# Graph layer on one core: edge tiles of 128 rows in place of 125, another first stage, whole scans over the edges' targets

## The chip, the cores and the metric

The kernel runs on one core of one Trainium2 chip. The metric is the device time of one execution in microseconds, the median of several runs.

## The reference

x is 6250 x 512, with 100,000 edges (src, dst) that are sorted by dst, and dst is dense at low numbers (the square of a uniform number). All is float32.

```python
xn = _layernorm(x, axis=-1)
# graph attention, 8 heads of 64
el = einsum('nhf,hf->nh', xn @ W_src + b_src, attn_l)
er = einsum('nhf,hf->nh', xn @ W_dst + b_dst, attn_r)
e = leaky_relu(el[src] + er[dst], 0.2)
a = exp(e - segment_max(e, dst)[dst]) / segment_sum(...)[dst]
gnn = segment_sum((xn @ W_val + b_val)[src] * a, dst)
# linear attention with random features: Q_phi, K_phi, V from xn @ Wq, Wk, Wv
mix = (Q_phi @ (K_phi^T V)) / (Q_phi @ sum(K_phi)) @ Wo
x = x + gnn + mix
# experts, top 781 tokens of each of 8 experts, after 8 Sinkhorn steps
out = x + ffn(_layernorm(x, axis=-1), gate_w, experts)
```

## The kernel before

Nodes lie in 50 tiles of P = 125; partition p of tile t holds node 50 p + t where tables are written by `by_tile`. Edges lie in ET = 800 tiles of 125, in sorted order. The stages, in order:

1. **First stage.** x comes in G = 25 groups of two tiles into six buffers (NXI). DVE takes mean and variance and normalizes, PE transposes into `xnT_all`, and multiplies by `welr`, the two logit weights folded with attn_l and attn_r (`fold_logit_weights` on DVE). Before the fold PE spreads four parameter rows over all partitions (`rows_spread`, L656 to L658). The logits el go to DRAM by group (`store_el`, L385 on SP's queue). SP loads the first six groups of x and the even ones after that (`load_x`, L379); ACT's queue loads the odd ones (L981). POOL meanwhile looks up where each node's edges begin (L537). `first_edge`, `all_edges` and `first_row` on DVE turn that into rows of the edge table; `first_row` needs one column moved by one partition, which a DMA on SP's queue does (L411, `starts_moved`), behind the loads of the projection weights (L398 to L406).
2. **Attention.** `group` on PE: 25 groups of projections (k, v, q, the graph values), feature maps and the sum over keys, and the values go to `val_tab` in DRAM (520 floats a row, 64 values and a one for each head). Then come the fold of Wo, the division (`divide`) and the output (`output`).
3. **Logit gathers.** Beside all this POOL issues one indirect DMA for each edge tile (`gather_logits`, L552): row src of `el_tab` to the partition of its edge. Edges are regarded as NCH = 16 chunks of CL = 6250, each of CT = 50 tiles; a gather goes to `ELP[:, g, c, :]`, for tile g of chunk c, and the order is by blocks of TB = 4 values of g (64 gathers), the last block first, NB = 13 blocks. After the first five blocks come 50 scatters of the er logits to the rows of `er_starts` where each node's edges begin (L565).
4. **Scans.** With the blocks turned by PE (`turn_block`), 128 partitions hold chunk and head, and 6250 columns the edges of a chunk. DVE copies the targets and compares neighbours (L1380, L1383), spreads er along equal targets by a scan (L1395), prepares two masks (L1398, L1400), all in 13 pieces, and then, block by block as logits come, adds, takes the leaky relu and the running maximum backwards (L1409 to L1414). A second pass (L1444 to L1447) subtracts the maximum, ACT takes the exponent, and PE turns the weights back to edge tiles.
5. **Edge loop.** POOL gathers `val_tab` rows for tile after tile into a ring of RING = 32 slots (`gather_pair`, L594), and reports a pair when it has landed, three pairs behind (`report`, L600, BEHIND = 3). DVE multiplies by the weights (`messages`, L1452 and L1463), ACT makes one-hot matrices of the targets (L1110, L1113), PE multiplies both (`block_sums`, L640) and sums into one of two accumulators for each of the 50 node blocks. `pairs` holds the pair at which a block ends; that pair is taken by both blocks. After each block come its gates (`gates`), a transpose (L892), the loading of the other two terms (`load_xm`) and a store (`store_x1`).
6. **Experts.** Sinkhorn, the choice of tokens, and 56 slots of 112 rows: an indirect read (L618), a product, an indirect write (L627).

```python
for u in range(ET // 2):
    eng.wait_ge(S["tile_free"], 2 * u + 2)
    gather_pair(u)
    if u >= BEHIND:
        report(u - BEHIND)
```

`chunk(...)`, `two(...)` and `mm(...)` are helpers for addresses in PSUM and matmuls; most matmuls carry the line of `mm`, L640.

## Time and profile before

| | us |
|---|---|
| median of 3 runs | 3210.87 (3203.05 to 3212.89) |
| profiled execution, its own time | 3184.74 |
| its span | 3182.6 |
| PE busy | 2569.4 |
| POOL busy | 2209.5 |
| DVE busy | 1621.1 |
| ACT busy | 993.6 |
| mean granted clock of PE | 0.907 |

The busy times are sums over the span and say little of what a stage waits for. The chain of waits follows the last instruction back to what released it, step by step; the windows give the busy time of each engine in each stage; the groups of lines give the mean of one instruction; and the rows of the timeline give each start and duration, with the idle time before it and what ended it.

### The profile page before, as it was taken

To read this page: it belongs to the slowest core of one execution; us is meant where nothing else is said; L and a number is where in the kernel's file an instruction comes from. 1 tells how busy PE (TensorE), PEld (TensorE's weight loads), DVE (VectorE), ACT (ScalarE), POOL (GpSimd) and SP (SyncE) were. 2 spreads that over 40 slices of the span, in tenths; PEclk is the share of its full clock that TensorE was granted. 3 is DMA by queue.
4 is the path that set the end of the run, shared out by engine and by line. 5 is a ranking of instruction groups with operands and counts; after the bars stand their busy time and mean duration, and the time that the engine had idled before them with its cause. 6 is when DMAs were issued, how large, how long until landed. Compare 5 with 4: busy or idle time off the path is not lost.

```text
span 3182.6 us, 47522 instructions
## 1 busy us (share of the span) xinstructions
PE 2569.4 (81%) x10463; PEld 1790.9 (56%) x10464; DVE 1621.1 (51%) x2963; ACT 993.6 (31%) x2564; POOL 2209.5 (69%) x1847
## 2 busy tenths in 40 slices
PE   6689999999999989951676777777888988934998
PEld 3366677776677744420454556665666766723443
DVE  6612222222222269985854555555666666767232
ACT  2312222222222210020454444554555655600111
POOL 6287778777778777877877877777777777600454
PEclk9889999999999989985699998898988999955999
DMA  4341121111111133420566667777777777630111
GB/s 144 122 105 33 31 37 29 29 29 29 30 31 29 23 105 119 117 64 3 157 174 173 176 181 183 185 186 182 194 193 187 196 193 195 175 111 0 45 52 38
DMA packets 276032, 341.23 MB, mean 107 GB/s; under 512 B 164855, under 2 KB 184030, under 8 KB 275850
## 3 DMA queue, kind: packets, MB, share of 16 engines
q0 software_dynamic: 218672, 227.51, 31.6%
q1 hardware_dynamic: 51709, 93.57, 9.1%
q10 hardware_dynamic: 5594, 19.52, 1.7%
q8 instruction: 20, 0.33, 0.0%
q14 instruction: 37, 0.30, 0.0%
HBM read 285.65 MB, written 55.25 MB: 107 GB/s over the span
## 4 chain that ended last, share of the span: by engine, by line
POOL 41%; PE 19%; issue 16%; DMA 13%; DVE 8%; DVEq 2%; POOLq 0%; ACT 0%; ACTq 0%
POOL R L552 31%; PE ps L640 17%; DMA R<-val_tab,src_i 11%; POOL R L594 8%; POOL er_starts L565 2%; DMA work<-in_x_dram 1%; DVEq L239 1%; DVE R L1463 1%; DVE work L1557 1%; DMA R<-in_L_gnn_b_dst_dram 1%; PE ps L934 1%; DVEq L1463 1%; PE ps L664 1%; DVE R L1444 0%; DVE R L1500 0%
## 5 line engine op out<-in xcount | busy, mean ns | idle before, releaser
L640 PE MATMUL ps<-R,work 125*125 (+3 forms) x5240 | 1650.6, 470 | 225.7 <-DVE R L1463 207.2
L640 PEld LDWEIGHTS ps<-R,work 125*125 125x125 f32 (+2 forms) x5240 | 987.6, 195 | 795.0 <-issue 655.7
L552 POOL DMA_INDIRECT R<-el_tab,src_i x800 | 984.6, 1231 | 341.1 <-issue 288.7
L594 POOL DMA_INDIRECT R<-val_tab,src_i x800 | 978.7, 1223 | 280.7 <-issue 180.8
L1463 DVE TENSOR_TENSOR R<-R,ps (+1 forms) x800 | 521.2, 693 | 131.4 <-DVE ps L1452 125.6
L1113 ACT ACTIVATE work<-work 125x125 f32<-125x125 f32 x900 | 277.8, 309 | 500.0 <-PE ps L640 472.1
L640 PE MATMUL ps<-work,R 128*128 128x250 f32 x1600 | 359.5, 383 | 21.8 <-DMA work<-R 21.8
L1110 ACT ACTIVATE work<-work,negdst 125x125 f32<-125x125 f32 x900 | 353.6, 393 | 59.2 <-issue 34.5
L640 PEld LDWEIGHTS ps<-work,R 128*128 128x128 f32 x1600 | 308.9, 194 | 59.1 <-issue 21.8
L1452 DVE COPY ps<-R (+1 forms) x401 | 69.9, 175 | 299.2 <-POOLq L600 227.1
L1295 DVE TENSOR_TENSOR R<-ps,R 125x512 f32<-125x512 f32 x50 | 34.6, 692 | 358.1 <-PE ps L640 358.1
L618 POOL DMA_INDIRECT R<-out_dram,work x56 | 55.7, 994 | 196.7 <-DVEq L1630 179.9
L1342 DVE RECIPROCAL work<-ps 128x1000 f32<-128x1000 f32 x25 | 160.0, 6402 | 13.0 <-PE ps L640 12.9
L640 PE MATMUL ps<-R 128*128 (+6 forms) x524 | 133.1, 402 | 26.8 <-DVEq L1626 13.6
L1166 ACT ACTIVATE work<-ps 128x448 f32<-128x448 f32 x56 | 30.4, 544 | 337.3 <-PE ps L934 337.3
L640 PEld LDWEIGHTS ps<-R 128*128 128x128 f32 (+3 forms) x524 | 83.3, 166 | 74.5 <-issue 34.6
L627 POOL DMA_INDIRECT out_dram<-R,work x56 | 54.0, 965 | 97.7 <-DVE R L1646 97.7
L1646 DVE SCALAR_TENSOR_TENSOR R<-ps,work,R 112x512 f32<-112x512 f32 x56 | 42.1, 751 | 149.8 <-PE ps L640 149.8
L1302 DVE TENSOR_SCALAR work<-ps 125x512 f32<-125x512 f32 x50 | 34.6, 692 | 157.1 <-PE ps L640 157.1
L1028 ACT ACTIVATE work<-ps 125x512 f32<-125x512 f32 x50 | 29.9, 597 | 246.5 <-PE ps L640 246.5
L640 PE MATMUL ps<-work 125*128 125x129 f32 (+1 forms) x500 | 74.1, 287 | 39.8 <-issue 38.4
L640 PE MATMUL ps<-omk,work 128*125 128x128 f32 x400 | 87.1, 309 | 21.4 <-DVE work L1303 21.4
(256 smaller groups left out, 2186.0 us busy)
## 6 DMA issues: line engine op xcount, KB each, us to landing
work<-in_x_dram SPq DMA_DIRECT2D x33, 500.0 KB
R<-el_tab,src_i POOLq DMA_INDIRECT x800
R<-val_tab,src_i POOLq DMA_INDIRECT x800, 5.9
val_tab<-R SPq DMA_DIRECT2D x50, 253.9 KB
work<-R SPq DMA_DIRECT2D x25, 500.0 KB
work<-xm_tab SPq DMA_DIRECT2D x50, 250.0 KB
out_dram<-R SPq DMA_DIRECT2D x50, 250.0 KB
xm_tab<-work ACTq DMA_DIRECT2D x17, 500.0 KB
```

The costliest lines, as they stand in the source:

```text
L552: eng.indirect_dma_start(out=ELP[:, g, c, :], out_offset=None, in_=el_tab[:, :], in_offset=bass.IndirectOffsetOnAxis(ap=src_i[:, t:t + 1], ...
L565: eng.indirect_dma_start(out=er_starts[:, :], out_offset=bass.IndirectOffsetOnAxis(ap=slot_s[:, t:t + 1], axis=0), in_=elr_all[:, 1, t, :] ...
L594: eng.indirect_dma_start(out=ring[:, slot, :], out_offset=None, in_=val_tab[:, :], in_offset=bass.IndirectOffsetOnAxis(ap=src_i[:, 2 * u + ...
L618: eng.indirect_dma_start(out=xs[q], out_offset=None, in_=out[:, :], in_offset=bass.IndirectOffsetOnAxis(ap=xs_tok[:, n:n + 1], axis=0), bo ...
L627: eng.indirect_dma_start(out=out[:, :], out_offset=bass.IndirectOffsetOnAxis(ap=xs_tok[:, n:n + 1], axis=0), in_=ys[q], in_offset=None, bo ...
L640: return pe.matmul(o, l, r, start=start, stop=stop)
L1110: fn(absd[s][0:P, :], iota_f[0:P, :], ACT.Abs, bias=negdst[:, bass.ds(2 * u + s, 1)]).then_inc(S["act_step"], 1)
L1113: fn(onehot[s][0:P, :], absd[s][0:P, :], ACT.Relu, scale=-1.0, bias=1.0).then_inc(S["onehot_ready"], 1)
L1342: st.done(v.reciprocal(rq.rearrange("p (b n) -> p b n", b=2), two(2 * b)))
L1452: v.tensor_copy(weights2[:, bass.ds(u % WPAIRS, 1), :].rearrange("p a h -> p (a h)"), EW2[:, bass.ds(u, 1), :].rearrange("p a h -> p (a h) ...
L1463: v.tensor_tensor(out=r3, in0=r3, in1=w_, op=ALU.mult).then_inc(S["msg_ready"], 1)
L1646: v.scalar_tensor_tensor(out=ys[m % NX], in0=ps[0:SLOT, 6 + m % 2, :], scalar=of_slot(2, n), in1=x_, op0=ALU.mult, op1=ALU.add).then_inc(S ...
```

## The change

- Edge tiles have B = 128 rows. A chunk has CT = 49 tiles and CL = 6272 edges, so that there are NT = 784 tile places, of which NE = 782 hold edges; the last two are skipped by the gathers. The last tile's empty rows have index 0 for src and no target. All tiles of stages 3 to 5 become 128 high. Node tiles stay at 125.
- `src_i` and `dst_i` arrive in another layout. The host's copy of src is for tiles of 125, so the indices are loaded on ACT's queue, cast, turned by PE, kept by DVE (`keep_rows`), written to DRAM (`src_nat`), read back as 112 rows of 896, turned by PE again (`turn_rows`) and kept. The targets are read from dst in 112 rows of 896 and turned by PE after the fold of Wo.
- The first stage: all x loads are on SP's queue; the parameter rows are loaded as broadcasts to 128 partitions on ACT's queue, and PE no longer spreads them; `first_edge` of the first half stands after three trips of six groups in place of two. The first row of each chunk and the gate weights are loaded on ACT's queue at the start. The zero fill of `er_starts` and the targets are loaded ahead of the one-column DMA.
- The scan of er and the two masks are one operation each over 6272 columns in place of 13 pieces.
- Attention's third buffer for x (NXM = 3) stays as it was.

```diff
-CL = E // NCH
-CT = CL // P
+B = 128
+CT = -(-E // (NCH * B))
+CL = CT * B
+NT = NCH * CT
+EQ = NT * B
+NE = -(-E // B)
+NI = 7
+NR = NT // NI
+REST = E - (NR - 1) * NI * B
...
             for g in range(NXI):
                 load_x(g)
+
+            eng.wait_ge(S["consts_ready"], 2)
+            eng.wait_ge(S["edge_rows"], 4)
+            n_ = (NI - 1) * 128 * P
+            eng.dma_start(src_nat[0:n_].rearrange("(j p n) -> p j n", p=128, n=P), src_turned[:, 0:NI - 1, :]).then_inc(S["idx_loaded"], 16)
+            eng.dma_start(src_nat[n_:E].rearrange("(p n) -> p n", n=P), src_turned[0:(E - n_) // P, NI - 1, :]).then_inc(S["idx_loaded"], 16)
+            eng.dma_start(src_nat[E:EQ].rearrange("(p n) -> p n", p=1), blank[0:1, 0:EQ - E]).then_inc(S["idx_loaded"], 16)
+            eng.wait_ge(S["idx_loaded"], 64)
+            eng.dma_start(src_rows, src_nat.rearrange("(p n) -> p n", p=NR)).then_inc(S["idx_loaded"], 16)
...
                 eng.dma_start(w_q, Wq.rearrange(wv4, p=128)).then_inc(S["proj_params"], 16)
+                eng.dma_start(er_starts.rearrange("(p a r) h -> p a (r h)", p=128, a=16),
+                              blank.unsqueeze(1).to_broadcast([128, 16, CT * H])).then_inc(S["er_zeroed"], 16)
+                eng.wait_ge(S["edge_psum"], 2)
+                eng.dma_start(dst_i[0:NR - 1, :], dst[0:E - REST].rearrange("(p n) -> p n", n=NI * B)).then_inc(S["heads_in"], 16)
+                eng.dma_start(dst_i[NR - 1:NR, 0:REST], dst[E - REST:E].rearrange("(p n) -> p n", p=1)).then_inc(S["heads_in"], 16)
...
                     for c in range(NCH):
                         t = c * CT + g
+                        if t >= NE:
+                            continue
...
-            for u in range(ET // 2):
+            for u in range(NE // 2):
                 eng.wait_ge(S["tile_free"], 2 * u + 2)
...
+            pe.wait_ge(S["edge_rows"], 7)
+            turn_rows(negdst_rows, 4)
...
-                        m = mm(halves_of[0], onehot[s][0:P, :], row[:, 0:DV // 2], False, stop)
+                        m = mm(halves_of[0], onehot[s], row[:, 0:DV // 2], False, stop)
...
-            for k in range(NB):
-                lo, hi = columns(k)
-                st.done(v.tensor_tensor_scan(out=scan_x[:, lo:hi], data0=scan_p[:, lo:hi], data1=scan_m[:, lo:hi],
-                                             initial=0.0 if k == 0 else scan_x[:, lo - 1:lo], op0=ALU.mult, op1=ALU.add))
-
-                st.done(v.tensor_scalar(scan_p[:, lo:hi], scan_p[:, lo:hi], -1.0, -FAR, ALU.add, ALU.mult))
-
-                st.done(v.tensor_scalar(scan_d[:, lo:hi], scan_d[:, lo:hi], ends[:, 2:3], FAR, ALU.subtract, ALU.mult))
+            st.done(v.tensor_tensor_scan(out=scan_x, data0=scan_p[:, 0:CL], data1=scan_m, initial=0.0, op0=ALU.mult, op1=ALU.add))
+
+            st.done(v.tensor_scalar(scan_p[:, 0:CL], scan_p[:, 0:CL], -1.0, -FAR, ALU.add, ALU.mult))
```

SP's queue at the start, before: eight loads of x, then stores of el between the even loads.

```order
L379 DMA work<-in_x_dram 125x1024 x8
L385 DMA el_tab<-negdst 125x16
L379 DMA work<-in_x_dram 125x1024
L385 DMA el_tab<-negdst 125x16 x2
L379 DMA work<-in_x_dram 125x1024
```

The same in the change:

```order
L396 DMA work<-in_x_dram 125x1024 x6
L410 DMA src_nat<-dst_i 128x6x125
L411 DMA src_nat<-dst_i 32x125
L412 DMA src_nat<-R 1x352
L414 DMA dst_i<-src_nat 112x896
L396 DMA work<-in_x_dram 125x1024 x4
L402 DMA el_tab<-negdst 125x16
```

The way of src through DRAM now stands between the sixth and the seventh load, and every later load of x is behind it.

SP's queue between the first stage and attention, before (`tb<-tb` is the one-column DMA, `work<-R` a group for PE):

```order
L406 DMA R<-in_L_mix_Wq_dram 128x4x512
L411 DMA tb<-tb 124x1
L417 DMA work<-R 128x4x250
L427 DMA gw<-in_L_ffn_gate_w_dram 128x4x8
L428 DMA smi<-in_dst_dram 16x1
L429 DMA dst_i<-in_dstT_dram 125x800
L430 DMA er_starts<-R 2000x1x400
```

The same in the change:

```order
L432 DMA R<-in_L_mix_Wq_dram 128x4x512
L433 DMA er_starts<-R 2048x1x392
L436 DMA dst_i<-in_dst_dram 111x896
L437 DMA dst_i<-in_dst_dram 1x544
L442 DMA tb<-tb 124x1
L448 DMA work<-R 128x4x250 x2
```

The zero fill and the targets moved from behind the one-column DMA and the first group to ahead of both.

## Rows read from the trace of the kernel before

**Rows 1.** The page, part 4: the chain that ended last, by engine and by line.
```profile
POOL 41%; PE 19%; issue 16%; DMA 13%; DVE 8%; DVEq 2%; POOLq 0%; ACT 0%; ACTq 0%
POOL R L552 31%; PE ps L640 17%; DMA R<-val_tab,src_i 11%; POOL R L594 8%; POOL er_starts L565 2%; DMA work<-in_x_dram 1%; DVEq L239 1%; DVE R L1463 1%; DVE work L1557 1%; DMA R<-in_L_gnn_b_dst_dram 1%; PE ps L934 1%; DVEq L1463 1%; PE ps L664 1%; DVE R L1444 0%; DVE R L1500 0%
```

**Rows 2.** Windows: busy PE, PEld, DVE, ACT, POOL; clock, DMA share, GB/s.
```profile
171.00:1381.00 1210.00, 1150.59 (x4612) 784.44 (x4612) 460.85 (x488) 217.87 (x305) 931.55 (x761) 0.98 0.23 52
...
1472.00:1510.00 38.00, 1.07 (x4) 0.71 (x4) 0.51 (x3) 0.00 (x0) 29.93 (x31) 0.50 0.09 3
...
1556.00:2178.00 622.00, 477.97 (x1955) 355.73 (x1956) 351.72 (x755) 314.96 (x965) 491.22 (x406) 0.95 0.69 180
2178.00:2797.00 619.00, 524.44 (x2335) 416.81 (x2334) 403.97 (x942) 352.39 (x1083) 450.26 (x368) 0.89 0.75 191
```

**Rows 3.** Timeline, end of the logit gathers: start, us, engine, line, [idle before].
```profile
1506.18 1.19 POOL L552 DMA_INDIRECT R<-el_tab,src_i  x1 [0.30 <-issue]
...
1508.81 1.07 PE L815 MATMUL ps<-ident,R 125*128 125x125 f32 x4 [44.87 <-DMA R<-el_tab,src_i]
...
1509.98 0.68 DVE L1409 TENSOR_TENSOR R<-R,ps 128x500 f32<-128x500 f32 x1 [37.49 <-PE ps L815]
```

**Rows 4.** Groups of POOL: busy us, mean ns | idle before.
```profile
L552 POOL DMA_INDIRECT R<-el_tab,src_i x800 | 984.6, 1231 | 341.1 <-issue 288.7 <-DMA el_tab<-negdst 52.5
L594 POOL DMA_INDIRECT R<-val_tab,src_i x800 | 978.7, 1223 | 280.7 <-issue 180.8 <-DMA R<-val_tab,src_i 57.1 <-PE ps L640 42.8
...
L618 POOL DMA_INDIRECT R<-out_dram,work x56 | 55.7, 994 | 196.7 <-DVEq L1630 179.9 <-issue 16.8
...
L559 POOL DMA_INDIRECT sm<-er_tab,smi x1 | 0.9, 862 | 0.3 <-issue 0.3
```

**Rows 5.** DMA issues: count, KB, median us to landing.
```profile
R<-val_tab,src_i POOLq DMA_INDIRECT x800, 5.9
...
R<-out_dram,work POOLq DMA_INDIRECT x56, 2.2
```

**Rows 6.** Waits in the edge loop, 1556 to 2797: us, times, longest.
```profile
POOL R L594 <- DMA R<-val_tab,src_i: 57.1, 126, 2.7
POOL R L594 <- PE ps L640: 42.8, 91, 2.8
```

**Rows 7.** First stage: two pieces of the chain, and DVE's statistics (groups, 0 to 160).
```profile
4.09 22.08 DMA R<-in_L_gnn_b_dst_dram
26.26 7.18 PE ps L640 x8
...
L1223 DVE BATCH_NORM_STATS2 work<-work 125x6 f32<-125x512 f32 x50 | 33.6, 673 | 15.4 <-DMA work<-in_x_dram 14.9 <-DVE tb L1200 0.2
```

**Rows 8.** Timeline between the first stage and attention.
```profile
150.36 0.43 SPq L398 DMA_DIRECT2D R<-in_L_mix_Wk_dram  x1
...
156.63 1.99 SPq L411 DMA_DIRECT2D tb<-tb  x1
...
167.10 2.16 SPq L430 DMA_DIRECT2D er_starts<-R  x1
...
169.85 0.16 DVE L1213 TENSOR_TENSOR tb<-tb 125x1 f32<-125x1 f32 x1 [15.40 <-DMA tb<-tb]
...
171.57 9.73 PE L640 MATMUL ps<-work,R 128*128 128x250 f32 x32 [21.77 <-DMA work<-R]
```

**Rows 9.** Timeline of DVE in the scans in pieces.
```profile
1404.43 1.28 DVE L1395 TENSOR_TENSOR_SCAN R<-R 128x500 f32<-128x500 f32 x1
1405.74 0.42 DVE L1398 TENSOR_SCALAR R<-R 128x500 f32<-128x500 f32 x1
...
1430.77 0.74 DVE L1395 TENSOR_TENSOR_SCAN R<-R 128x250 f32<-128x250 f32 x1
1431.54 0.29 DVE L1398 TENSOR_SCALAR R<-R 128x250 f32<-128x250 f32 x1
```

**Rows 10.** Timeline of PE late in the loop: after a block, and five pairs.
```profile
2736.51 0.94 PE L640 MATMUL ps<-gw,work 128*125 128x8 f32 x8
...
2738.22 9.03 PE L640 MATMUL ps<-R,work 125*125 x40
```

More of the change, by code:

```diff
@@ L65, in block_tiles @@
 def block_tiles(k):
-    return NCH * (min(TB * k + TB, CT) - TB * k)
+    return sum(c * CT + g < NE for g in range(TB * k, min(TB * k + TB, CT)) for c in range(NCH))
 def logits_by(k):
@@ L519, in _ @@
             eng.sem_inc(S["consts_ready"], 1)
-            for t_ in (ident[:, :], halves[:, :], half2[:, :], before[:, :], EW2[:, ET // 2, :]):
+            for t_ in (ident[:, :], halves[:, :], half2[:, :], before[:, :]):
                 st.done(eng.memset(t_, 0.0))
@@ L606, in _ @@
                     report(u - BEHIND)
-            for u in range(ET // 2 - BEHIND, ET // 2):
+            for u in range(NE // 2 - BEHIND, NE // 2):
                 report(u)
@@ L650, in _, with turn_rows @@
             pe.wait_ge(S["consts_ready"], 2)
-            pe.wait_ge(S["elr_params"], 96)
-            pe.wait_ge(S["row_ready"], 1)
-            for r in range(4):
-                last = mm(ps[:, 4 + r, :], ones[0:1, :], s_rows[:, r, :])
-            last.then_inc(S["rows_spread"], 1)
+            pe.wait_ge(S["edge_rows"], 1)
+            for j in range(NI):
+                n_ = min(128, ET - 128 * j)
+                last = pe.transpose(ps[0:n_, 4 + j // 4, (j % 4) * P:(j % 4) * P + P], src_f[:, 128 * j:128 * j + n_], ident[0:P, 0:P])
+            last.then_inc(S["edge_psum"], 1)
+            def turn_rows(rows_, b):
+                for i in range(NI):
+                    last = pe.transpose(ps[:, b + i // 4, (i % 4) * NR:(i % 4) * NR + NR], rows_[:, B * i:B * i + B], ident[0:NR, 0:NR])
+                last.then_inc(S["edge_psum"], 1)
             def turn(g, s):
@@ L680, in turn_back @@
                     pe.wait_ge(S["elr_ready"], g - 1)
[L681 to L682 removed]
+                if isinstance(g, int) and g == 0:
+                    pe.wait_ge(S["edge_rows"], 6)
                 pe.sem_inc(S["pe_passed"], 1)
@@ L691, in trip @@
                     turn(g, b)
+                    if isinstance(g, int) and g == 1:
+                        pe.wait_ge(S["row_ready"], 1)
+                        pe.wait_ge(S["idx_loaded"], 80)
+                        turn_rows(src_rows, 6)
                     if not isinstance(g, int) or g >= 1:
@@ L992, in copy_logits, with trip @@
                     .then_inc(S["elr_ready"], 1)
-            def trip(i, more=True):
+            def trip(i):
                 for b in range(NXI):
@@ L998, in trip @@
                     copy_xT(g, b % 2)
-                    if more and b % 2:
-                        load_x(g + NXI, b)
                     if not isinstance(g, int) or g >= 1:
@@ L1008, in _ @@
             trip(0)
-            with act.Fori(1, G // NXI - 1) as i:
+            with act.Fori(1, G // NXI) as i:
                 trip(i)
-            trip(G // NXI - 1, False)
             copy_xT(G - 1, 0)
@@ L1423, in _ @@
             v.wait_ge(S["iota_ready"], 1)
-            st.done(v.tensor_scalar(cmp[0:T, :], ps[0:T, 4, 0:ET // 2], thr[0:T, :], 0.0, ALU.add, ALU.is_gt))
+            st.done(v.tensor_scalar(cmp[0:T, :], ps[0:T, 4, 0:NT // 2], thr[0:T, :], 0.0, ALU.add, ALU.is_gt))
             st.done(v.tensor_reduce(out=cnt[0:T, 0:1], in_=cmp[0:T, :], axis=AX.X, op=ALU.add))
```

180 lines of the change are left out of this document (99 added, 81 removed).

## Prediction

> **What bounds the kernel now.** I read the chain that ended last first, then the stages, then the ends of the waits in each. Over the whole span the chain is POOL's more than anyone's, and two lines carry it, the logit gathers (L552) and the value gathers (L594) [rows 1]. By stages [rows 2]:
> - 171 to 1381 us, attention: PE is busy 1151 of 1210 us at a clock of 0.98. POOL gathers logits beside it.
> - 1472 to 1510: every other engine is idle. DVE waits 37.49 us for PE, PE waited 44.87 us for the logits' DMA, and the last logit gather was issued at 1506.18 [rows 3]. This is all of POOL's first queue that lies on the path.
> - 1556 to 2178 and 2178 to 2797, the edge loop: 406 and 368 gathers, so 1.53 and 1.68 us for one, against 1.503 us that POOL needs for a gather in steady state (1.20 busy, 0.30 between [rows 3]); the mean is 1.223 + 0.30 = 1.52 [rows 4]. POOL lost only 57 us to landings and 43 us to PE [rows 6]. PE has slack in the first half (478 of 622) and little in the second (524 of 619).
> - After 2797 nothing is changed.
>
> **Indirect DMA, its price by rows.** Every change to the two gathers hangs on what one with 128 rows costs POOL. Four groups bear on it [rows 4]: 16 rows 862 ns, 112 rows 994, 125 rows 1231 and 1223. From 16 to 112 the price grows by 0.13 us, from 112 to 125 by 0.23. So it isn't the number of rows alone: 125 is costly in a way that 16 and 112 are not, and these two are multiples of 16, as 128 is. Landings split the same way: 2.2 us for 112 rows of 2 KB, 5.9 for 125 of 2080 bytes [rows 5]; the second figure is under more load. On the first slope 128 rows cost 0.994 + 16 x 0.13/96 = 1.02 us. The bounds are 0.99 (112 rows) below and 1.223 + 3 x 0.018 = 1.28 above (the slope from 112 to 125 continued). The nearest row by count is the 125's; I take 1.02, because the kink can't come from count.
>
> The Trainium skill (DMA: Bandwidth & Descriptors, on why a DMA increments its semaphore by 16) says that a DMA is spread over the largest number of engines up to 16 that divides the slow dimension of both sides: 16 for 128 or 112 rows, 5 for 125. The trace agrees with it in both jumps. By that rule the sum is the one I give, 3055; by the nearest row in count it would be rival C or D, 3155 or 3249.
>
> **The change, part by part** (against the profiled run's own 3184.7 us).
> 1. Start, loads on ACT's queue. Broadcasts to 128 partitions (4 x 256 KB) and the source indices (391 KB) join 2 MB of weights, of which the last parameter took 22.08 us; the rows' spread on PE (7.18 us) goes [rows 7]. The fold starts at 33.5 now; 1.4 MB more at 2 MB per 22 us is up to +15, less 7 is +8, and if they are hidden -7. I take +2.
> 2. Start, SP's queue. Four transfers that carry the source indices through DRAM stand between the 6th and the 7th load of x, and SP waits for them in order. The first six loads cover the time until the fold is done, then x is needed at once. DVE lost 14.9 us to x in this stage [rows 7]. So some is hidden; bounds 0 and 15, I take +3. Seven transposes and five copies on PE and DVE lie in the wait for the parameters.
> 3. Start of attention. PE began at 171.57, after DVE had waited 15.40 us for the one-column DMA, queued at 156.63 behind weights from 150.36 on: 4.35 MB in 19.5 us, 0.22 MB/us [rows 8]. Now the zero fill (3136 KB) and the targets (391 KB) stand ahead of it: 3.5 MB at 0.22 is +16, issue alone (2.16 for such a fill) +2; the fill now has 128 slices in place of 125, so I take +12.
> 4. Targets are turned on PE at the end of attention: three small DVE operations, 7 transposes, 2 copies in place of one operation. Most lies beside the fold's work on PE and ACT; +2 (0 to 5).
> 5. Whole scans. Thirteen pieces of three operations now: the second began at 1404.43, the last, half as wide, at 1430.77 [rows 9], so 2.39 us each and 30.4 in all. A scan of 500 columns takes 1.28, one of 250 0.74: 2.16 ns a column, 13.7 for 6272; the second operation grows by 0.52 ns a column (0.42 to 0.29), 3.4, and I take the third for the same. 20.6 in place of 30.4: -10. What is left of a piece for the third, with gaps, is 0.69; if its whole cost scales, it is 8.6 and the sum -5. Bounds -3 and -11.
> 6. Logit gathers: 18 fewer, and 782 at 1.02 + 0.30. POOL began at 152.4; 782 x 1.34 + the 51 transfers for the targets' logits (80 us) end near 1290. At 1.21 it would still be about 1481, where DVE is due at 1472 + 19 - 10 = 1481. So the 37.5 us of rows 3 go: -37.5. What is late next is DVE's own chain, and that is the cover of this part.
>    Parts 1 to 6: +17 + 2 - 10 - 37.5 = **-28.5**.
> 7. Value gathers. First half (14 blocks): 622 us for 406 tiles now. It becomes 396 tiles; POOL's floor is 1.32, I add 0.02 for slow ones as now and 0.05 for waits: 396 x 1.39 = 550, and 4 of the ring's 32 slots more are filled before the loop (27 are now): 545, so **-77**. Second half: 368 become 359 tiles, POOL's floor 359 x 1.34 = 481. PE's floor: 40 matmuls of five pairs take 9.03 us, the gates, transposes and zeroing of a block 1.9 more [rows 10]; PE's 524 busy us at a clock of 0.89, less 9 tiles (10 us), are 514, or some 465 at 0.99. With both floors near 480 and small blocks that keep them from overlapping, I take 570: **-49**. Together -126, from 0 (price as by count) to -180 (both halves at the larger floor).
> DVE and ACT are busy for 352 and 315 of the first 622 us, 404 and 352 of the last 619 [rows 2], and neither gets more to do.
>
> Sum: -28.5 - 126 = -154.5, 3030 on the profile's scale. That run is 0.8% below the median of the runs shown (3210.87); on the median's scale, 3030 x 1.0082 = **3055**.
>
> **Rivals** (on the median's scale; a measurement here can tell 0.3%, 10 us, from no change).
> - A, as above: 2985 to 3100. For: rows 4 and 5, and PE's slack. Chance 0.60.
> - B, the price falls, but the loop finds another bound. DMA engines are busy 0.69 to 0.75 of the time [rows 2]; a gather that is spread over all 16 lands when its slowest engine is done, among them those that copy x rows in 125-row transfers for each block. POOL waits for a landing three pairs back, 7.9 us at the new pace, where it was 9; a landing of 8.5 us would hold the pace at 1.42. The loop then gains about 60: 3184.7 - 28.5 - 60 = 3096, **3121**. Against: landings take 5.9 now. 0.17.
>   The Trainium skill (DMA: Bandwidth & Descriptors, latency and other measured facts) says that two of the sixteen engines are usually slower, which would hurt just a gather that uses all; no row here shows single engines. By it B would gain weight and the sum stay.
> - C, the price is one of the instruction, flat at 1.21: parts 1 to 6 as above, the loop gains 18 x 1.52 = 27: 3129, **3155**. 0.12.
> - D, slower: the price grows by rows at the slope from 112 to 125, to 1.28. The place is POOL's queue, twice. Logits: 782 x 0.055 = 43 more, less 18 x 1.66 = 30, and POOL starts 5 later: the last lands near 1524, so the start is +18, not -28.5. Loop: 782 x 1.58 = 1236 against 800 x 1.52 = 1216, +20. In all +38: 3223, **3249**. It decides from about 1.24, where both gains are used up. Against: 16 to 112 rows, which cost almost nothing. 0.08.
> - E, the price falls but the start loses 50 more, as x stands still for the detour: **3105**. 0.03.
>
> **Numbers.** Time 3055, the likeliest case. Range 2985 to 3135: A, B and E, leaving out C and D (0.20). Faster by over 0.3%: A, B, C, E, 0.92. D's price can fall between 1.21 and 1.28: 0.02 within 0.3%, 0.06 slower.
>
> **What would show it.** Gathers of about 1.02 us busy and landings under 4 us show the price; 1.21 or more kills A. No wait of PE for the logits' DMA at the end of the DVE scans, POOL idle there. Three long DVE operations of about 13.7, 3.4 and 3.4 us. First attention matmul near 188. Loop about 1115 us, over 400 gathers in its first 560 us; waits of POOL for PE, not DMA, in the second half. If instead POOL's waits for landings grow well above 57 us, it is B. A gather of 1.02 with a loop above 1180 would make my second half wrong, and the first matmul after 200 my start.

## The result, and the profile after

| | us |
|---|---|
| changed kernel, median of 4 | 4219.39 (4218.59 to 4221.32) |
| kernel before, median of 4 | 3209.64 (3203.05 to 3212.89) |
| ratio | 1.315, 95% interval 1.313 to 1.317 |
| predicted | 3055 (2985 to 3135), 0.92 for faster |

The prediction is wrong in its sign. The changed kernel is slower by 1010 us. The same file, run beside the kernel before in one of the experiments below (g_after), took 2975.56 us against 3170.60, a ratio of 0.938 (0.935 to 0.941). Both numbers are real. What happens in the slow case, and what sets it off, is the subject of this part.

First the price on which the prediction hung. Groups of POOL in the changed kernel (busy us, mean ns | idle before):
```profile
L579 POOL DMA_INDIRECT R<-el_tab,src_i x782 | 799.0, 1022 | 243.7 <-issue 243.1 <-POOL R L569 0.6
L621 POOL DMA_INDIRECT R<-val_tab,src_i x782 | 754.5, 965 | 657.8 <-PE ps L667 351.5 <-issue 174.4 <-remote 70.2
```
They answer to [rows 4]: 1.02 and 0.97 us in place of 1.23 and 1.22. POOL did what was forecast, and in the second queue it now waits 352 us for PE, where it lost 43 to it [rows 6].

The loss is beside POOL. Windows of the changed kernel (busy PE, PEld, DVE, ACT, POOL; clock, DMA share, GB/s); the first two lie in attention, the last two are the edge loop:
```profile
190.00:400.00 210.00, 38.02 (x114) 25.64 (x114) 4.92 (x16) 5.24 (x8) 159.14 (x166) 0.55 0.08 6
...
1400.00:1600.00 200.00, 191.32 (x837) 138.61 (x836) 49.25 (x78) 43.20 (x61) 0.00 (x0) 0.99 0.09 30
2471.00:3040.00 569.00, 429.61 (x1597) 314.05 (x1598) 303.17 (x646) 259.85 (x797) 336.55 (x354) 0.88 0.62 172
3040.00:3840.00 800.00, 635.53 (x2629) 492.03 (x2627) 448.75 (x1041) 396.77 (x1218) 385.48 (x399) 0.87 0.57 167
```
Before, PE was busy 95% of attention with the logit gathers beside it [rows 2]. Now it is busy 38 us of 210 while they run, and 191 of 200 as soon as they have ended (POOL 0.00). DVE and ACT starve with it: 16 and 8 instructions in 210 us. The DMA engines are not the reason; their share is 0.08.

What the starved engines wait for, 180 to 2100 us (us, times, longest):
```profile
PEld ps L667 <- issue: 1113.5, 831, 90.0
PE ps L667 <- issue: 822.6, 143, 87.9
DVE R L1339 <- remote: 523.5, 5, 109.5
...
ACT work L1073 <- remote: 264.4, 3, 88.2
POOL R L579 <- issue: 238.5, 766, 1.6
```
"Issue" is a wait for nothing that the profile shows, "remote" for something it can't name. They are not semaphores: a matmul inside a group of matmuls waits for none. The timeline shows it on both sides:
```profile
355.38 0.94 POOL L579 DMA_INDIRECT R<-el_tab,src_i  x1 [0.30 <-issue]
356.63 0.94 POOL L579 DMA_INDIRECT R<-el_tab,src_i  x1 [0.31 <-issue]
356.79 0.37 PE L667 MATMUL ps<-work,R 128*128 128x250 f32 x1 [0.50 <-issue]
357.88 0.94 POOL L579 DMA_INDIRECT R<-el_tab,src_i  x1 [0.30 <-issue]
358.18 0.19 PEld L667 LDWEIGHTS ps<-work,R 128*128 128x128 f32 x1 [2.08 <-issue]
359.12 0.94 POOL L579 DMA_INDIRECT R<-el_tab,src_i  x1 [0.30 <-issue]
359.58 0.37 PE L667 MATMUL ps<-work,R 128*128 128x250 f32 x1 [2.43 <-issue]
```
POOL issues a gather every 1.25 us without a flaw, and PE gets one matmul in 2.8 us. It isn't an even slowing: with the same gathers beside it PE was busy 8.3 us of the 8.5 up to 356.5, and from 300 to 345 it did nothing at all. I call this state **starved**: the other engines' instructions issue only now and then, in bursts with long gaps, while POOL's gathers run.

The account: POOL issued the last logit gather at 1346.7 us, and most of attention's work was then still to be done, alone. The first value gather came at 2423.4, where before it came at 1510.9: +912 up to the loop. From there to the end it is 4217.0 - 2423.4 = 1794, before 3182.6 - 1510.9 = 1672: +122. Together that is the difference of the two profiled spans, 1034. The profiled execution of the kernel before (3184.74 us) lies below all four of its timed runs above, and nothing on record says whether it met the same conditions as they did.

### The profile page after: what moved, and what is told of

The parts are those of the page before. It is cut to its first block, busy times and chain, and to the rows that moved or that the text cites. A ratio compares the mean times of both kernels' runs of the same rounds, so it can differ in the third digit from the quotient of the medians.

```text
span 4217.0 us, 47008 instructions
## 1 busy us (share of the span) xinstructions
PE 2699.7 (64%) x10400; PEld 1849.1 (44%) x10401; DVE 1602.6 (38%) x2908; ACT 981.6 (23%) x2528; POOL 1800.3 (43%) x1810
## 2 busy tenths in 40 slices
DMA packets 160455, 341.55 MB, mean 81 GB/s; under 512 B 54509, under 2 KB 69733, under 8 KB 160270
## 3 DMA queue, kind: packets, MB, share of 16 engines
q0 software_dynamic: 101376, 225.55, 20.7%
## 4 chain that ended last, share of the span: by engine, by line
PE 47%; another core or an unknown queue 19%; issue 15%; DVE 11%; POOL 2%; DMA 2%; ACT 1%; DVEq 1%; ACTq 1%; SPq 1%; POOLq 0%
PE ps L667 46%; DVE work L1393 4%; POOL R L621 2%; DMA work<-in_x_dram 1%; DMA R<-in_L_gnn_b_dst_dram 1%; PE ps L970 1%; DVE work L1603 1%; ACT work L1149 1%; ACT work L1146 0%; PE ps L928 0%; DVE R L1458 0%; PE ps L695 0%; ACTq L1005 0%; DVE R L1490 0%
## 5 line engine op out<-in xcount | busy, mean ns | idle before, releaser
L667 PE MATMUL ps<-R,work 128*125 (+3 forms) x5168 | 1745.6, 493 | 409.0 <-issue 273.6
L667 PEld LDWEIGHTS ps<-R,work 128*125 128x125 f32 (+1 forms) x5168 | 1022.5, 206 | 1037.4 <-issue 889.0
L621 POOL DMA_INDIRECT R<-val_tab,src_i x782 | 754.5, 965 | 657.8 <-PE ps L667 351.5
L579 POOL DMA_INDIRECT R<-el_tab,src_i x782 | 799.0, 1022 | 243.7 <-issue 243.1
L667 PE MATMUL ps<-work,R 128*128 128x250 f32 x1600 | 383.8, 395 | 259.4 <-issue 158.0
L1149 ACT ACTIVATE work<-work 128x125 f32<-128x125 f32 x882 | 272.2, 309 | 634.0 <-PE ps L667 336.2
L1146 ACT ACTIVATE work<-work,negdst 128x125 f32<-128x125 f32 x882 | 346.6, 393 | 53.8 <-issue 29.7
L667 PEld LDWEIGHTS ps<-work 125*128 125x128 f32 (+1 forms) x500 | 61.9, 194 | 326.3 <-issue 326.1
L667 PEld LDWEIGHTS ps<-omk,work 128*125 128x125 f32 x400 | 65.9, 202 | 301.7 <-issue 281.0
L645 POOL DMA_INDIRECT R<-out_dram,work x56 | 55.8, 997 | 220.1 <-DVEq L1676 203.4
L1357 DVE TENSOR_TENSOR kvacc<-kvacc,ps 128x516 f32<-128x516 f32 x25 | 17.3, 692 | 287.9 <-PE ps L667 121.0
```

The source lines that it names most:

```text
L579: eng.indirect_dma_start(out=ELP[:, g, c, :], out_offset=None, in_=el_tab[:, :], in_offset=bass.IndirectOffsetOnAxis(ap=src_i[:, t:t + 1], ...
L621: eng.indirect_dma_start(out=ring[:, slot, :], out_offset=None, in_=val_tab[:, :], in_offset=bass.IndirectOffsetOnAxis(ap=src_i[:, 2 * u + ...
L645: eng.indirect_dma_start(out=xs[q], out_offset=None, in_=out[:, :], in_offset=bass.IndirectOffsetOnAxis(ap=xs_tok[:, n:n + 1], axis=0), bo ...
L667: return pe.matmul(o, l, r, start=start, stop=stop)
L1146: fn(absd[s], iota_f, ACT.Abs, bias=negdst[:, bass.ds(2 * u + s, 1)]).then_inc(S["act_step"], 1)
L1149: fn(onehot[s], absd[s], ACT.Relu, scale=-1.0, bias=1.0).then_inc(S["onehot_ready"], 1)
```

## Experiments

The runs came in ten batches. Each batch has the kernel before beside it, run on the same chip in the same minutes. "Clean" is a run without starvation. The batches e, f, h, i and j have one run of each kernel, the others two to seven.

| runs of one batch | chip | before | changed kernel or control | place |
|---|---|---|---|---|
| the result | - | 3209.6 | 4219.4 | starving |
| e1 to e4 | 5 | 3171.8 | none in the batch | clean |
| c_after, c_zeroed | 12 | 3278.5 | 4251.0, 4243.7 | starving |
| f1 to f4 | 4 | 3191.8 | none in the batch | clean |
| g_after, g_paced, g_b112 | 8 | 3170.6 | 2975.6 | clean |
| h1_mixed | 7 | 3197.8 | first phase starved | starving |
| i1_mixed | 13 | 3269.6 | last phases starved | starving |
| j1_paces | 4 | 3173.4 | unpaced values fast | clean |
| j2_paces | 12 | 3175.9 | unpaced values fast | clean |
| k1_paced | 8 | 3199.9 | unpaced values slow | starving |

### Rows, spread and pace, without a control (e1 to e4)

e1: both gathers fetch 125 rows. e2: 25 rows for the logits. e4: the kernel before, with 112 rows.
```
-  eng.indirect_dma_start(out=ELP[:, g, c, :], ... ap=src_i[:, t:t + 1] ...
+  eng.indirect_dma_start(out=ELP[0:125, g, c, :], ... ap=src_i[0:125, t:t + 1] ...
```
e3: all 128 rows, with a small memset behind each logit gather that POOL waits for.
```
+  st.done(eng.memset(pad[:, :], 0.0))
```


> The changed kernel, whose two gathers (logits on L579, values on L621) fetch 125 of a tile's 128 rows; the first 32 value tiles are still whole. Three rows of nearly every tile are left out of the sums; ELP is zeroed first (some 5 us of POOL). Everything else, the number of gathers (782) too, is as changed. Theory H1 (how the 128 rows are spread over the DMA engines starves the other engines' instruction supply) and H2 (POOL's faster pace, 1.25 to 1.30 us a gather, does it): both say that the price goes back to 1.22 us and the pace to 1.51, PE is busy for some 190 us in 200 again in 190 to 800 us, attention ends as before, the edge loop takes 782/800 of the 1241 us before, 1213, and the whole is 3210 + 13 (start) - 10 (scans) - 37 (22 gathers fewer, taken as wholly on the path at 1.51 in each half: 33 and 33 at most) = 3140 to 3215 us. H3 (the loss comes from something else of the change: first stage, addresses, whole scans, the order of SP's queue): it stays near 4200 us, with PE starved from 208 us on.

> The changed kernel, whose logit gathers (L579) fetch only 25 of 128 rows of each tile (the rest of ELP is zeroed first); value gathers as changed. The packets then go over 5 DMA engines as those of 125 rows did, but POOL is fast: I expect a price near 0.9 us and a pace near 1.2. H1 (spread over all 16 engines): attention runs at full PE speed, 190 us busy in 200, although POOL's pace is 1.2; the loss of the attention stage (some 880 us) is gone and only that of the loop stays: 3210 + 130 = about 3300 to 3400 us. H2 (POOL's pace): attention is starved as in the changed kernel or worse, about 4100 to 4250 us.

> The changed kernel with one small memset (128x4), awaited, behind each logit gather of 128 rows, which brings POOL's pace there from 1.25 to some 1.45 to 1.55 us; value gathers as changed. H2 (pace): attention is at full speed or nearly, total about 3300 to 3450 us with the loop's loss alone. H1 (spread): attention stays starved while the gathers last, and they last longer: 782 x 0.2 = 160 us more of it, 4150 to 4400 us.

> The kernel before, whose gathers (logits and, from the 33rd tile on, values) fetch 112 of a tile's 125 rows; 13 rows of a tile are left out of the sums. Still 800 of each. Price expected near 1.00 us and pace 1.25 to 1.3. H1 and H2 both: the old kernel falls into the same state, PE starved from the start of attention until the gathers end near 1180 us, total 3900 to 4200 us. H3 (something else of the change): the old kernel gets faster or stays, 3050 to 3210 us.

Measured: 3148.65, 2976.13, 2979.03 and 2973.45 us, before 3171.82. PE was busy 191 to 192 of 200 us from 400 to 600 in all four. e4 has the fast gathers in the old kernel and is clean, against H1 and H2; e2 has them in the changed one, where both asked for 3300 us or more, and is clean too; e3 has all of the rest of the change and is clean, against H3. All three theories seemed to fall at once. The experiment lacked the one run that could have said why: the changed kernel itself.

### The control (c_after, c_zeroed)

> The changed kernel unchanged, run beside the one before on the chip on which the first four experiments ran (the kernel before took 3172 us there). Those four left out rows or paced POOL and all ran without starvation, the paced one with all 128 rows. If the starvation belongs to 128-row gathers issued back to back (theory T: rows and pace together), it is here again: 4200 us, PE starved from 208 us. If it belongs to the chip or to the moment (theory C), this takes about 2960 to 2990 us, as the paced kernel with its 2979 us, whose attention stage doesn't end later than the one of this kernel could.

> The changed kernel with nothing but the small memset ahead of the logit gathers (128x16) made one over all of ELP (128x6272), as in the experiments with fewer rows: the gathers keep 128 rows and their pace. Theory T (128 rows back to back): 4200 us. Theory P (the place of POOL's instructions or the later start of its gathers decides, so that any small edit ends the starvation): 2960 to 3000 us here, 4200 us for the unchanged one. Theory C (chip or moment): both about 2960 to 3000 us.

Measured: 4250.96 and 4243.68 us, before 3278.53. In c_after PE was busy 38.27 us (x114) of 190 to 400, beside 38.02 (x114) in the first profile: the same starvation to the instruction, in another batch. At this point I took it for a property of 128 rows issued back to back, which was one reading too far: the chip had changed too, from that of e1 to e4.

### Early or late, rows, and the value gathers alone (f1 to f4)

f1 and f2: the small memset of e3 only behind the late or only behind the early logit gathers. f3: logits of 120 rows. f4: values of 112 rows, logits as changed.
```
+  if k < NB - EARLY:        # f1;  k >= NB - EARLY in f2
+      st.done(eng.memset(pad[:, :], 0.0))
```


> The changed kernel with the small awaited memset of e3 behind the logit gathers only after the er scatters; the some 270 gathers before them are back to back. In e3 all of them were paced and nothing starved, and the loop's value gathers, not paced, ran clean as well (1.25 to 1.35 us each), though the changed kernel's loop starved with the same code. Theory L (latched: once starvation has set in, the program stays prone to it to its end): starved 208 to 511 us, clean or partly starved in the paced part, and the edge loop slow as in the changed kernel (1370 us), in all 3500 to 3700 us. Theory M (each moment for itself: it needs unpaced 128-row gathers at that time): starved only until about 511 us, that is some 250 us lost to 2979, hidden in nothing: 3200 to 3260 us, the loop fast (1000 us).

> The reverse: the some 270 logit gathers before the er scatters paced, the 512 behind them back to back. Theory M: clean until about 600 us, starved then for 512 x 1.3 = 660 us, and the loop fast: 2979 + 550 to 650 = 3500 to 3650 us. Theory S (it sets in only at the start of attention, when the other engines' programs are first loaded beside POOL's gathers): clean throughout, 2970 to 2990 us. Theory L: as M but with the slow loop too, 3850 to 4000 us.

> The changed kernel with logit gathers of 120 of 128 rows, back to back (8 rows of each tile are left out; ELP is zeroed first). 112 rows back to back were clean at 1.27 us a gather (88 rows a us), 128 rows paced to 1.38 (93 a us) too, 128 at 1.25 (102 a us) starved. Theory R (a limit on rows per us, between 93 and 102): 120 rows at some 1.27 us are 94 a us, clean or just starved. Theory K (it takes exactly 128 rows, a whole partition width, or 8 rows on each of 16 DMA engines): clean, 2970 to 2990 us. If starved: 4150 to 4250 us.

> The changed kernel with the logit gathers as they are (starved) and value gathers of 112 rows from the 33rd tile on (16 rows of a tile left out). Theory L (latched): the loop is slow all the same, about 1370 us, total 4150 to 4250 us. Theory M (own cause): the loop takes some 1010 us as in e4, total about 4217 - 360 = 3830 to 3880 us.

Measured: 2973.51, 2977.53, 2971.80 and 2975.91 us, before 3191.83. No theory had f4: its logit gathers are those of the changed kernel, 128 rows every 1.25 us, and PE was busy 199 of the 210 us from 190 to 400. A later stage can't mend an earlier one, so I took what differed to lie outside the kernel, which the next batch tests.

### The same chip for kernel and variants (g_after, g_paced, g_b112)

> The changed kernel, unchanged, on the same chip and in the same minutes as the next two. So far it starved wherever it was run (4219 us, and 4251 us on the chip of the two controls), while all eight variants, run on two other chips, were clean, even the one that changed only the value gathers and left the logit gathers as they are. So chip and kernel are confounded. Theory C (the chip decides: on some chips back-to-back 128-row gathers starve the other engines, on others not): on a clean chip this takes 2970 to 2980 us, on a starving one 4200 to 4250 us. Theory E (the exact program decides): 4200 to 4250 us, with the next two clean.

> The kernel of e3 again (an awaited small memset behind each logit gather), 2979 us there. Theory E: 2980 us on any chip. Theory C: 2980 us on a clean chip; on a starving chip, where pace matters if anything does, it shows whether 1.38 us a gather is enough: 2980 to 3100 us if it is, over 4100 us if it isn't, and its unpaced value loop starves there as the changed kernel's, 350 us more.

> The kernel of e4 again (the kernel before with 112-row gathers; 13 rows of a tile left out), 2973 us there. Theory E: 2975 us on any chip. Theory C: 2975 us on a clean chip; on a starving chip it shows whether 112 rows at 1.27 us starve the others too, over 4000 us, or stay clean.

Measured: 2975.56, 2978.10 and 2977.46 us, ratios 0.938 (0.935 to 0.941), 0.939 (0.936 to 0.942) and 0.939 (0.936 to 0.942). The unchanged changed kernel is clean here. So theory C holds, with a correction that came later: chip 12 was starving for the controls and clean for j2_paces, chip 8 clean here and starving for k1_paced. It isn't the chip alone, but the core on it or the moment, and the record can't part these two; I call it the **place**. e1 to f4 had met clean places and told nothing of what starves.

This clean run is also the test of the prediction's own terms. The chain by engine, groups, DMA issues and windows of g_after:
```profile
PE 53%; DVE 18%; DMA 11%; issue 9%; DVEq 4%; POOL 4%; SPq 1%; ACTq 1%; ACT 0%; POOLq 0%
```
```profile
L579 POOL DMA_INDIRECT R<-el_tab,src_i x782 | 751.9, 962 | 238.7 <-issue 238.0 <-POOL R L569 0.6
L621 POOL DMA_INDIRECT R<-val_tab,src_i x782 | 751.1, 960 | 366.1 <-issue 167.2 <-PE ps L667 95.6 <-PE ps L852 56.3
```
```profile
R<-val_tab,src_i POOLq DMA_INDIRECT x782, 3.9
```
```profile
193.00:1240.00 1047.00, 991.19 (x4204) 706.57 (x4205) 311.95 (x424) 217.88 (x305) 789.52 (x807) 0.98 0.17 38
1487.00:2036.00 549.00, 463.63 (x1979) 349.15 (x1979) 376.98 (x795) 326.67 (x984) 402.25 (x419) 0.93 0.75 213
2036.00:2590.00 554.00, 490.57 (x2284) 391.51 (x2285) 387.67 (x924) 344.49 (x1057) 340.42 (x356) 0.94 0.71 210
```
POOL has left the chain (41% before [rows 1], 4% now) and PE has taken it; landings fell from 5.9 to 3.9 us [rows 5]; the loop's windows moved 213 and 210 GB/s where they moved 180 and 191 [rows 2]. The first of them begins 37 us ahead of the loop's first product, at 1523.7.

### Phases in one kernel (h1_mixed)

Since the place can't be chosen, the kernel has to carry its own control: the forms of gather stand in phases, 128 rows back to back among them. The value gathers have phases too: 128, 112, 128 with the memset, and 125 rows.
```
+  n_ = 112 if k in (6, 7) else 125 if k in (2, 3) else 64 if k < 2 else 128
+  eng.indirect_dma_start(out=ELP[0:n_, g, c, :], ... ap=src_i[0:n_, t:t + 1] ...
+  if k in (8, 9):
+      st.done(eng.memset(pad[:, :], 0.0))
```


> The changed kernel with its gathers in phases, so that one run carries its own control, whatever chip it gets. Logits, in order of time: 144 tiles of 128 rows back to back (170 to 350 us), 128 of 128 rows with the awaited memset behind each, the er scatters, 128 of 112 rows, 128 of 128 rows back to back, 128 of 125 rows, 128 of 64 rows. Values: tiles 0 to 195 of 128 rows, then 112 rows, then 128 with the memset, then 125 rows. The rows not fetched are left out of the sums (ELP is zeroed first). Theory C (the chip decides): on a clean chip PE is 190 us busy in 200 throughout and the whole takes about 3000 us. On a starving chip the first phase starves (PE under 40 us busy in 200), and each later phase tells its own form: R (rows per us decide): clean while paced, at 112, 125 and 64 rows, starved again only in the second back-to-back phase, in all 3300 to 3400 us; L (any fast gather): starved in all phases but that of 125 rows, over 3700 us.

Measured: 4132.19 us, before 3197.78. A starving place. Its windows: 128 rows; 128 with the memset; the er scatters; 112; 128; 125; 64 rows; POOL idle:
```profile
190.00:340.00 150.00, 21.00 (x64) 14.53 (x64) 1.77 (x8) 3.78 (x4) 113.41 (x121) 0.55 0.08 6
345.00:535.00 190.00, 59.64 (x160) 36.12 (x160) 9.51 (x15) 7.94 (x11) 131.23 (x245) 0.62 0.07 7
570.00:645.00 75.00, 71.82 (x318) 52.12 (x317) 18.79 (x30) 16.58 (x24) 58.34 (x49) 1.00 0.18 31
650.00:800.00 150.00, 41.93 (x100) 21.36 (x98) 3.85 (x9) 3.96 (x7) 113.14 (x122) 0.57 0.07 5
810.00:975.00 165.00, 30.90 (x75) 19.03 (x76) 5.97 (x6) 2.67 (x3) 126.00 (x123) 0.54 0.08 8
985.00:1170.00 185.00, 21.16 (x66) 15.62 (x66) 3.85 (x9) 3.96 (x7) 144.60 (x119) 0.52 0.10 5
1180.00:1330.00 150.00, 19.83 (x44) 10.00 (x43) 0.69 (x1) 2.50 (x3) 113.23 (x121) 0.52 0.06 7
1400.00:1500.00 100.00, 95.96 (x423) 70.56 (x422) 27.14 (x43) 23.10 (x33) 0.00 (x0) 0.98 0.07 23
```
R falls: neither fewer rows nor the memset ended it, though with the memset PE was busy 60 us of 190, over twice its share in the first phase. L (any fast gather) has its number, "over 3700", but not its exception: the 125-row phase starved too, 21 us busy in 185, at 1.21 busy and 0.30 between, the very pace at which the kernel before is clean. Either a starved phase carries over into the next, or the changed program is vulnerable by another part. Only the scatters, 50 in 77 us behind a pause of POOL of 27 us, were clean. In the value loop 195 gathers took 311 us with 128 rows, 324 with 112, 331 with 128 and the memset, and the 193 with 125 rows 308; form and place in the loop are mixed there, and it decides nothing.

### 125 rows first (i1_mixed)

```
+  n_ = 125 if k >= 6 else 112 if k >= 3 else 128
```


> The changed kernel in phases again, now with 125 rows from the start: logits of 125 rows for the some 270 tiles before the er scatters and the 128 behind them, then 192 tiles of 112 rows, then 192 of 128; values 32 tiles whole, of 125 rows up to tile 391, of 128 behind. Rows not fetched are left out (ELP is zeroed first). In the phased run before, on a starving chip, the phase of 125 rows starved too (PE 27 us busy in 199), though the kernel before, with 125 rows throughout, ran clean on that chip. On a clean chip: 3060 to 3110 us, clean throughout, nothing told. On a starving chip: theory L (latched by the first fast gathers): the 125-row phases are clean (PE 190 busy in 200 from 193 to some 800 us), starvation begins with the 112-row phase or, if 112 rows are still slow enough, with the 128-row phase, and the whole takes 3450 to 3700 us. Theory P (the changed program is vulnerable whatever the rows, by something else than the gathers' form): starved from 208 us on, over 4100 us.

Measured: 3751.66 us, before 3269.60. Windows: 125 rows, up to the scatters; 125 rows, behind them; 112; 128; then in the loop 125 and 128:
```profile
193.00:560.00 367.00, 349.86 (x1524) 254.64 (x1525) 91.23 (x149) 81.63 (x115) 285.34 (x233) 0.98 0.18 31
650.00:870.00 220.00, 210.46 (x936) 155.04 (x936) 57.87 (x89) 49.26 (x70) 170.23 (x139) 0.99 0.18 31
886.00:1110.00 224.00, 36.94 (x87) 21.51 (x88) 6.43 (x8) 5.30 (x7) 169.51 (x178) 0.52 0.07 4
1115.00:1380.00 265.00, 41.80 (x94) 22.20 (x94) 8.05 (x12) 5.30 (x7) 204.64 (x189) 0.53 0.07 6
2124.00:2429.00 305.00, 226.50 (x848) 150.52 (x846) 159.40 (x333) 139.77 (x428) 238.03 (x196) 0.96 0.67 175
2600.00:3100.00 500.00, 394.06 (x1595) 303.05 (x1594) 270.06 (x619) 244.16 (x751) 261.81 (x271) 0.88 0.58 167
```
Theory L (latched), and this is the run that shows what sets it off. With 125 rows PE is busy 350 of 367 and 210 of 220 us in the changed program. The first gather of 112 rows starts at 871.76:
```profile
870.24 1.21 POOL L580 DMA_INDIRECT R<-el_tab,src_i  x1 [0.30 <-issue]
871.76 0.95 POOL L580 DMA_INDIRECT R<-el_tab,src_i  x1 [0.31 <-issue]
873.01 0.95 POOL L580 DMA_INDIRECT R<-el_tab,src_i  x1 [0.30 <-issue]
```
There is one every 1.24 to 1.25 us from there; PE works on in full until 885, and then it is busy 37 of 224 us. In the result it was the same: PE began at 193 beside the fast gathers, was busy 14 of 15 us up to 208 and 3 of the next 32. The total missed its range upward by 50. On such a place it takes the fast gathers to start the starvation; all the rest of the change, in force from the start, doesn't. Whether the fast gathers alone are enough isn't shown: the kernel before with 112 rows (e4, g_b112) met clean places only. A starved phase does carry over: 125 rows starve behind a starved phase (h1) and not from a clean start (here). The value loop goes the same way, more mildly: 196 gathers in 305 us with 125 rows, 271 in 500 with 128.

### Pace or form (j1_paces, j2_paces, k1_paced)

125 rows are slower, and their gathers also have another form: 125 rows go over 5 DMA engines instead of 16 if the spread taken in the prediction holds, which no run shows. To part the two: 128 rows throughout, whole computation, with two, one and no awaited memsets behind a gather (j1, j2), and with two behind every logit gather and none behind the values (k1).
```
+  for _ in range(2):        # j1, j2: 2, then 1, then 0, and so for the values
+      st.done(eng.memset(pad[:, :], 0.0))
```


> The changed kernel, whole computation, 128 rows everywhere, with awaited small memsets (128x4) behind each gather, two of them at first, then one, then none: logits two for the some 380 tiles of blocks 7 to 12, one for the 320 of blocks 2 to 6 and none for the last 128; values two up to tile 255, one up to 511, none behind. One memset brought the logit pace from 1.27 to 1.38 us, two should give some 1.55. In i1, on a starving chip, 125 rows at 1.57 us were clean, and 112 rows at 1.25 starved at once. On a clean chip: 3000 to 3060 us, nothing told. On a starving chip: theory V (pace alone: what decides is how long POOL leaves between gathers): clean with two memsets until some 800 us; with one, at 1.38, either; starved in the last phase (165 us, some 130 us of them lost); in all 3150 to 3450 us. Theory W (the form: the descriptors of 125 rows, over 5 DMA engines, are what is safe; 128 rows aren't at any such pace): starved from 208 us on, PE under 60 us busy in 200 while the gathers last, 4300 us or more.

> The kernel of j1_paces once more, unchanged: that run got a clean chip (3195 us, PE 94 to 96 busy in 100 through all three paces) and so told nothing of a starving one. On a clean chip again: 3190 to 3200 us. On a starving chip, theory V (pace alone decides): clean at two memsets (1.55 us a gather) until some 750 us; with one memset, at 1.38, either; starved in the last phase; in all 3300 to 3500 us. Theory W (the form decides, 128 rows starve at such paces too): starved from 208 us on, PE under 60 us busy in 200 while the gathers last, 4300 us or more.

> The changed kernel, whole computation, with two awaited small memsets behind each logit gather (1.55 us a gather instead of 1.27) and value gathers left as changed, back to back: a version that might do on either kind of core. The same kernel as before met a clean core on chip 12, where the changed kernel had starved, so it isn't the chip alone but the core or the session that decides; I call it the place. The kernel before took 3171 to 3192 us on the clean places and 3198 to 3278 on the starving ones. On a clean place: logits end near 1400 us, beside the scans, and their pace costs up to 30 us against the 2976 of the changed kernel: 2980 to 3010 us. On a starving place, theory V (pace decides): attention clean (PE 190 busy in 200), the loop slow by its unpaced values (1350 us against 1010): 3310 to 3400 us; theory W (the form decides): starved from 208 us on, 4300 us or more.

j1 and j2: 3195.07 and 3198.21 us, before 3173.38 and 3175.85. Clean places twice, so nothing on starvation, as foreseen, and one thing beside: with value gathers slowed too, the whole gain was gone.

k1: 3269.78 us (3265.69 to 3291.10), before 3199.92, ratio 1.024 (1.020 to 1.028). A starving place, which its values show. Attention, and the loop in two windows:
```profile
193.00:1177.00 984.00, 929.41 (x4036) 674.63 (x4037) 250.99 (x395) 217.90 (x305) 763.16 (x1804) 0.98 0.16 34
1487.00:2077.00 590.00, 435.18 (x1597) 314.67 (x1597) 326.91 (x665) 266.32 (x799) 352.64 (x369) 0.86 0.63 173
2077.00:2880.00 803.00, 636.65 (x2672) 491.11 (x2672) 452.62 (x1054) 404.44 (x1242) 391.63 (x405) 0.89 0.57 165
```
Two of its gathers and what stands between them:
```profile
299.76 0.95 POOL L580 DMA_INDIRECT R<-el_tab,src_i  x1 [0.27 <-POOL pad L583]
...
300.71 0.27 POOL L583 MEMSET pad<- 128x4 f32 x2
...
301.26 0.95 POOL L580 DMA_INDIRECT R<-el_tab,src_i  x1 [0.27 <-POOL pad L583]
```
Theory V in attention: 128 rows, 0.95 us busy, but 1.50 us from one to the next, and PE is busy 929 of 984 us. The form isn't needed to be safe: 128 rows are safe too when POOL leaves this room. That the place would have starved the unslowed gathers rests on the loop of the same runs. The kernel is some 950 us better than the changed one in the result. The loop takes back more than the rest of the change gives: the unpaced values take from 1475.1 to 2825.7, 1351 us, against 1060 in g_after (1476.2 to 2536.1) and 1257 before (1510.9 to 2767.6). The total came 40 us under the expected range, since I had priced a clean loop at 1010 us: with g_after's 1060 the loop's loss is 291 and not 340, and 2976 + 291 = 3267.

## Why the prediction was wrong, and where it was right

The step that failed is part 6, with part 7 behind it: POOL's gathers were made faster and **the work beside them was taken to go on as it had**. The text took up what POOL waits for and what waits for POOL, and "neither gets more to do" for DVE and ACT. It never asked what a POOL that issues every 1.25 us in place of 1.50 does to engines that share nothing with it in the program. The net loss, +912 before the loop and +122 from there, is that: POOL's own price fell as forecast (1.02 us), but PE was busy 38 us of 210 beside the gathers, where part 6 had it go on at its pace of before (1151 of 1210 [rows 2]).

No row of before shows it, and that was the warning: no stage had gathers at under 1.50 us with other engines at work beside them. The only fast ones, 112 rows [rows 4], stand in a stage in which POOL mostly waits. The price was bounded from both sides, its effect on others not at all, and rival D, the only slower one, priced POOL alone.

Point by point, on a clean place (g_after; its span 2976.2 against 3182.6 of the profile of before, 206 us less, where 154.5 were forecast on that scale):
- Parts 1 to 3, first attention matmul forecast near 188: 194.43 (192.93 on record). Right in kind, 6 us short.
- Part 5, whole scans, 13.7 and 3.4 us: right.
```profile
1419.95 13.22 DVE L1439 TENSOR_TENSOR_SCAN R<-R 128x6272 f32<-128x6272 f32 x1
1433.21 3.43 DVE L1441 TENSOR_SCALAR R<-R 128x6272 f32<-128x6272 f32 x1
```
- Part 6, logit gathers end near 1290: the last was issued at 1229, and DVE waited for no logits. It added the last block at 1480.4, where the prediction had it due at 1481, in place of 1509.98: 30 us gained, forecast 28.5. The first value gather came 35 us earlier, at 1476.2 in place of 1510.9.
- Part 7, from the first value gather to the first row read of the last stage (L645, L618 before): 1266 us, before 1438, so 172 gained; forecast 126. Mis-sized: the price (0.96, not 1.02) and the waits added to it, in the first half: from the first product at 1524 on, 413 gathers in 533 us are 1.29 us for one (1.39 in the forecast), the next 340 in 533 are 1.57 (1.59). A gather took 1060/781 = 1.36 us on average, 1257/799 = 1.57 before. From 1487 to 2590 POOL lost 40.6 us to landings and 95.6 to PE (57.1 and 42.8 before [rows 6]), the sign that the prediction gave for A. The rest of the span, 234 us, is the same in both.
- Rival B spoke of landings that a spread over all 16 engines would hold up; they fell to 3.9 us, under the 4 asked for.
- The reason given for the price is not shown. The Trainium skill's rule (DMA: Bandwidth & Descriptors, on why a DMA increments its semaphore by 16) gives 16 engines for 128 and 112 rows, and the prices agree: 0.96 us for 128 rows, as for 112 and unlike 125 (1.22). But by the same rule 25 rows go over 5 engines, as 125 do, and e2's gathers of 25 rows cost 0.96. So neither 5 engines alone nor a count of rows that isn't a multiple of 16 makes a gather costly. What does part 125 rows from the others is the count of packets in POOL's queue: 101376 in the changed kernel, in e2 and in f3 (logits of 25 and of 120 rows), but 209376 in e1, in which 1532 gathers fetch 125 rows. That is some 70 more for each; why they need more is open.

Its ratio of 0.951 was too timid for a clean place (0.938) and has the wrong sign for a starving one (1.315). Of the ten batches, the result's among them, five met a starving place, so neither number alone is the kernel's. On both kinds the kernel before is the steadier: 3171 to 3192 us on clean places, 3198 to 3279 on starving ones. No trace of the kernel before is known to come from a starving place, so where its own loss of up to some 100 us arises is not shown.

**Open.** What starves the engines: the waits have no releaser in the profile, and no count of bytes or packets differs between c_after and g_after (160455 packets, 341.55 MB in each). What makes a place starving. Whether the kernel before would starve with fast gathers there. Whether one awaited memset from a clean start is enough (h1 had it only behind a starved phase). Whether pace as such or POOL's awaited stop between two gathers helps. A version with the logits slowed and 125 rows, or slowed 128, for the values was not run on a starving place; on a clean one it would give most or all of the gain back (j1 3195.07, and e1 with 125 rows in both 3148.65, beside 3173.38 and 3171.82). So no version here beats the kernel before on every place: on clean ones the changed kernel does, by 6.2%.

## What to carry to other kernels

Work that a stage hides was hidden here only while its issue left the others room: when you make a hidden queue of indirect DMAs faster, price what runs beside it at the new pace too, and where no row shows that pace, keep a slower case with real weight. Put the unchanged kernel into every batch of variants; where a run can't choose its place, put the forms to be compared into phases of one kernel, the suspected one last, because the state it started here outlived it. When a faster queue has slack, as the logits' has here (it ended some 190 us before the scans), slowing it on purpose cost nothing on a clean place (2978.10 beside 2975.56 us) and saved the stage on a starving one.

## What the runs showed of the hardware that was not expected

- On starving places, indirect gathers at 1.24 to 1.25 us from one to the next cut PE to 37 busy us in 224, DVE and ACT likewise, at a DMA share of 0.07. At 1.50 to 1.57 us the same engines are undisturbed (350 of 367 and 929 of 984 us). On clean places 1.25 to 1.28 us disturbs nobody.
- It starts with 112 rows as with 128. Once begun, it went on through gathers of 64 rows, and through those of 125 at 1.21 + 0.30 us, which are harmless from a clean start; 125-row scatters behind a pause of POOL of 27 us were clean.
- It is reproducible to the instruction in different batches (PE x114 in 190 to 400 us, twice; the chip of the first is not on record), and chips 8 and 12 each showed both kinds of place in different batches.
- TensorE's granted clock followed, it didn't cause: 0.52 to 0.57 in starved windows (0.62 in the phase with the memset), near the lower of its two levels (1.2 and 2.4 GHz), and 0.98 as soon as POOL was idle.
